# Output stage of a transformer layer: tiles in pairs, in another order, with shared small operations

## The reference

```
x = layernorm(x + attention(x, Wqkv, Wo))          # 16 heads of 16, rotary positions
normed = x * rsqrt(mean(x^2) + 1e-8) * norm_weight
shared = relu(normed @ sw1 + sb1) @ sw2 + sb2      # hidden size 1024
comb   = the two best of 8 experts a row, by sigmoid(normed @ router_w.T), weights normalised
routed = sum over the two: comb * (relu(normed @ ew1[e] + eb1[e]) @ ew2[e] + eb2[e])
out    = layernorm(x + shared + routed)            # (v - mean) / sqrt(var + 1e-5)
```

## Time and profile before

| | |
|---|---|
| median of 3 runs | 1319.67 us (1319.3 to 1321.2) |
| the profiled execution's own time | 1322.56 us |
| its span in the trace | 1320.7 us |
| mean granted clock of TensorE | 0.97 |
| busy: TensorE, VectorE, ScalarE, GpSimd | 1220.1, 1028.5, 970.0, 578.8 us |
| `combine` | about 1234 us to the end, 87 us |
| last product of TensorE | 1291.4 us |

### The profile page before, as it was taken

How to read it: one execution, slowest core, us unless ns; L and a number is a source line. 1 busy time by engine, 2 the same in 40 slices (tenths; PEclk the granted TensorE clock), 3 DMA queues, 4 the chain that set the end, 5 groups by cost and what they waited for, 6 DMA issues and landing times.

```text
span 1320.7 us, 29483 instructions
## 1 busy us (share of the span) xinstructions
PE 1220.1 (92%) x9377; PEld 933.8 (71%) x9440; DVE 1028.5 (78%) x2009; ACT 970.0 (73%) x1938; POOL 578.8 (44%) x572
## 2 busy tenths in 40 slices
PE   4799999999999999869999969999999999999991
PEld 3444444444444444238899969999999999999891
DVE  5788887888788878629756638888888888888798
ACT  4599998999899999747744427767767677677684
POOL 5332322232223210007436645666666666666560
PEclk9899999999999999999899989999999999999996
DMA  9300101010000000442022246777777777776344
GB/s 298 107 18 2 34 9 29 2 34 2 20 2 18 2 18 18 141 135 69 14 89 90 85 132 222 251 251 238 245 238 242 241 239 239 245 249 203 127 146 139
DMA packets 125412, 161.25 MB, mean 122 GB/s; under 512 B 17088, under 2 KB 108224, under 8 KB 125312
## 3 DMA queue, kind: packets, MB, share of 16 engines
q1 hardware_dynamic: 118496, 141.25, 33.2%
q0 software_dynamic: 6816, 18.75, 3.7%
HBM read 122.06 MB, written 37.52 MB: 121 GB/s over the span
## 4 chain that ended last, share of the span: by engine, by line
PE 75%; DMA 9%; DVE 8%; issue 3%; ACT 3%; POOL 1%; SPq 0%; another core or an unknown queue 0%; ACTq 0%; DVEq 0%; POOLq 0%
PE att_psV L387 9%; PE att_psA L330 9%; PE att_psB L340 8%; DMA slots_x<-sent_rows,all_slot 6%; PE exp_psU L1581 5%; PE exp_psU L1583 5%; PE exp_psU L1582 5%; PE exp_psD L1566 5%; PE exp_psD L1567 5%; PE exp_psD L1568 5%; PE att_psT L354 4%; PE att_psX L408 2%; PE att_psX L410 2%; PE att_psX L409 2%; PE exp_psT L1554 1%
## 5 line engine op out<-in xcount | busy, mean ns | idle before, releaser
L529 DVE TENSOR_REDUCE att_mx<-att_psA 128x1 f32<-128x512 f32 x512 | 337.6, 682 | 76.3 <-PE att_psA L330 74.9
L445 ACT ACTIVATE att_prob<-att_psB 128x512 f32<-128x512 f32 x512 | 299.3, 599 | 54.1 <-PE att_psB L340 40.0
L1626 ACT ACTIVATE exp_psU<-exp_psU,ew_b 128x256 f32<-128x256 f32 x312 | 126.9, 445 | 132.2 <-PE exp_psU L1583 132.2
L330 PE MATMUL att_psA<-att_qk 96*128 96x512 bf16 x512 | 197.5, 388 | 6.4 <-DVE att_mx L529 2.4
L340 PE MATMUL att_psB<-att_qk 128*128 128x512 bf16 x449 | 172.4, 386 | 14.1 <-issue 5.4
L1566 PE MATMUL exp_psD<-exp_w2h,exp_hh 128*128 128x256 f32 x624 | 175.7, 282 | 0.0
L1581 PE MATMUL exp_psU<-exp_xh,exp_w1h 128*128 128x256 f32 x624 | 173.7, 278 | 1.4 <-DVE exp_xl L1650 1.4
L1583 PE MATMUL exp_psU<-exp_xh,exp_w1l 128*128 128x256 f32 x624 | 173.3, 278 | 0.0
L1582 PE MATMUL exp_psU<-exp_xl,exp_w1h 128*128 128x256 f32 x624 | 173.3, 278 | 0.0
L1567 PE MATMUL exp_psD<-exp_w2l,exp_hh 128*128 128x256 f32 x624 | 172.4, 276 | 0.0
L1568 PE MATMUL exp_psD<-exp_w2h,exp_hl 128*128 128x256 f32 x624 | 172.3, 276 | 0.0
(11 more groups left out here) (203 smaller groups left out, 3240.3 us busy)
## 6 DMA issues: line engine op xcount, KB each, us to landing
ew_w<-ew SPq DMA_DIRECT2D x40, 1024.0 KB, 7.0
exp_w<-ew SPq DMA_DIRECT2D x38, 1024.0 KB, 7.1
slots_x<-pre_acc SPq DMA_DIRECT2D x13, 780.0 KB, 10.5
pre_spare<-slots_x SPq DMA_DIRECT2D x39, 260.0 KB, 5.5
out_g<-rows_y SPq DMA_DIRECT2D x32, 256.0 KB, 3.1
ew_b<-eb SPq DMA_DIRECT2D x39, 128.0 KB, 5.9
pre_spare<-xT SPq DMA_DIRECT2D x8, 512.0 KB, 4.5
attn_rows<-att_ob SPq DMA_DIRECT2D x8, 512.0 KB, 2.8
```

Of the source, the lines that this page charges most:

```text
L330: pe.matmul(psA[A_BANK[n % U]][:, :], r[:, 0, qt * P:(qt + 1) * P], r[:, 1, :], start=True, stop=True).then_inc(s_amm, 1)
L445: act.activation(prob[:, n % PR, :], psB[B_BANK[n % U]][:, :], ACT.Exp, scale=SCALE).then_inc(s_exp, 1)
L529: dve.reduce_max(mx[:, g % 2, n % U:n % U + 1], psA[A_BANK[n % U]][:, :], AX_X).then_inc(s_max, 1)
```

## The change

`combine` now works on pairs of tiles, numbered k = 0 to 15 in the order ORDER = 0, 1, 2, 11, 3, 4, 12, 5, 6, 13, 7, 8, 14, 9, 10, 15 (pair p holds tiles 2p and 2p+1; 11 to 15 are the blocks whose shared product is made here).

- VectorE: the first sum of both tiles, one wait, the second sum of both, one wait, the statistics of both, one wait, two aggregates. One reciprocal and one scaled mean over two columns serve both. They belong to pair k-2 up to k = 8, to pairs 7 and 8 at k = 9, and to pair k-1 after that. The add of block n stands directly before its own pair. All eight `hidden_lo` of block 0 come before `rows_lo` of block 1; `rows_lo` of block 2 comes after pair 0.
- ScalarE: one root for two tiles, in slots given by the list ROOT; two normalisings in slots given by NORM. The relus and `rows_hi` keep their slots, and roots of a slot come before its normalisings.
- GpSimd: the same instructions in the same order.
- SP: the load of pair i+6 waits until pair i is summed, and the stores follow three pairs behind.
- y, o and the small buffers hold six pairs in place of eight tiles.

```diff
+    R, LAG = 6, 2
+    ORDER = list(range(3))
+    for n in range(NB):
+        ORDER += [EARLY + n] + list(range(2 * n + 3, min(2 * n + 5, EARLY)))
+    ROOT = [6, 8, 10, 12, 14, 15, 18, 19] + [12 + k for k in range(8, PAIRS)]
+    NORM = [10, 12, 14, 16, 18, 19, 20, 21] + [13 + k for k in range(8, PAIRS)]
...
+            def add_up(k):
+                p, r = ORDER[k], k % R
+                dve.wait_ge(s_g[r], 32 * (k // R + 1))
+                if k >= R:
+                    dve.wait_ge(s_o, 2 * (k - R + 1))
+                if p >= EARLY:
+                    dve.wait_ge(shared.added, p - EARLY + 1)
+                for t in range(2):
+                    i = 2 * p + t
+                    ins = dve.scalar_tensor_tensor(y[:, r, t, :], g[:, r, 0, t, :], m.gate[:, 0, i:i + 1], m.acc[:, i, :], ALU.mult, ALU.add)
+                link(ins)
+                for t in range(2):
+                    i = 2 * p + t
+                    ins = dve.scalar_tensor_tensor(y[:, r, t, :], g[:, r, 1, t, :], m.gate[:, 1, i:i + 1], y[:, r, t, :], ALU.mult, ALU.add)
+                ins.then_inc(s_y, 1)
+                dve.wait_ge(s_y, k + 1)
+                dve.bn_stats(st[:, r, 0, :], y[:, r, 0, :])
+                link(dve.bn_stats(st[:, r, 1, :], y[:, r, 1, :]))
+                for t in range(2):
+                    dve.bn_aggr(mv[:, r, t, :], st[:, r, t, :]).then_inc(s_var, 1)
+
+            def scale(k):
+                r = k % R
+                dve.wait_ge(s_sd, k + 1)
+                link(dve.reciprocal(sd[:, r, 1, :], sd[:, r, 0, :]))
+                dve.scalar_tensor_tensor(sd[:, r, 2, :], mv[:, r, :, 0], -1.0, sd[:, r, 1, :], ALU.mult, ALU.mult).then_inc(s_nm, 1)
...
             shared.rows_lo(dve, Nth(0))
-            for slot in range(LAG + TILES + 2):
...
+            for h in range(shared.HC):
+                shared.hidden_lo(dve, Nth(0), h)
+            rows_ahead(1)
+            for k in range(PAIRS):
+                n = ORDER[k] - EARLY
+                if n >= 0:
+                    shared.add(dve, Nth(n))
+                add_up(k)
+                if k == 0:
+                    rows_ahead(2)
+                if n >= 0:
+                    rows_ahead(n + 3)
+                if LAG <= k < PAIRS - 7:
+                    scale(k - LAG)
+                if k == PAIRS - 7:
+                    scale(k - 2)
+                if k >= PAIRS - 7:
+                    scale(k - 1)
+            scale(PAIRS - 1)
...
+            def root(k):
+                r = k % R
+                act.wait_ge(s_var, 2 * (k + 1))
+                act.activation(sd[:, r, 0, :], mv[:, r, :, 1], ACT.Sqrt, bias=eps[:, 0:1]).then_inc(s_sd, 1)
...
+            for i in range(PAIRS + 3):
+                if i + R < PAIRS:
+                    sp.wait_ge(s_y, i + 1)
+                    load(i + R)
+                if i >= 3:
+                    k = i - 3
+                    for t in range(2):
+                        row = (2 * ORDER[k] + t) * P
+                        sp.wait_ge(s_o, 2 * k + t + 1)
+                        sp.dma_start(out[row:row + P, :], o[:, k % R, t, :]).then_inc(s_st[k % R], 16)
```

More of the change, by code:

```diff
@@ L1703, in combine @@
     TILES = T // P
[L1704 to L1707, removed]
+    PAIRS = TILES // 2
+    EARLY = m.early_blocks
+    NB = PAIRS - EARLY
+    R, LAG = 6, 2
+    HP = m.sb1.shape[1] // 2
+    SLOTS = NB * HP
+    ORDER = list(range(3))
+    for n in range(NB):
+        ORDER += [EARLY + n] + list(range(2 * n + 3, min(2 * n + 5, EARLY)))
+    assert sorted(ORDER) == list(range(PAIRS))
+    ROOT = [6, 8, 10, 12, 14, 15, 18, 19] + [12 + k for k in range(8, PAIRS)]
+    NORM = [10, 12, 14, 16, 18, 19, 20, 21] + [13 + k for k in range(8, PAIRS)]
     with ExitStack() as ctx:
@@ L1711, in combine @@
         eps = given.eps
[L1712 to L1720, removed]
+        g = a.sb("g", [P, R, 2, 2, D], F32)
+        y = a.sb("y", [P, R, 2, D], F32)
+        o = a.sb("o", [P, R, 2, D], F32)
+        st = a.sb("st", [P, R, 2, 6], F32)
+        mv = a.sb("mv", [P, R, 2, 2], F32)
+        sd = a.sb("sd", [P, R, 3, 2], F32)
+        shared = Shared(a, m, 2 * EARLY, buffers=2)
+        s_g = [a.sem(f"outputs_loaded{i}") for i in range(R)]
         s_var = a.sem("variance")
@@ L1728, in combine @@
         block = pr.block
[L1730 to L1733, removed]
         @block.gpsimd
         def _(pool):
-            for slot in range(TILES + 2):
-                n, h = divmod(2 * (slot - 1), shared.HC)
-                if n == 1 and h == 0:
+            for n in range(1, NB):
+                if n == 1:
                     pool.wait_ge(shared.lo_ready, shared.HC)
-                if 1 <= n < NB:
+                for h in range(shared.HC):
                     shared.hidden_lo(pool, Nth(n), h)
-                    shared.hidden_lo(pool, Nth(n), h + 1)
         @block.vector
@@ L1754, in _, with rows_ahead @@
+            def scale(k):
[3 more added lines that the diff above has]
+                dve.scalar_tensor_tensor(sd[:, r, 2, :], mv[:, r, :, 0], -1.0, sd[:, r, 1, :], ALU.mult, ALU.mult).then_inc(s_nm, 1)
+            def rows_ahead(n):
+                if n < NB:
+                    shared.rows_lo(dve, Nth(n))
             pr.after_last(dve)
             shared.rows_lo(dve, Nth(0))
-            for slot in range(LAG + TILES + 2):
[L1757 to L1784, removed]
@@ L1796, in _, with normalise @@
         def _(act):
+            def root(k):
+                r = k % R
+                act.wait_ge(s_var, 2 * (k + 1))
+                act.activation(sd[:, r, 0, :], mv[:, r, :, 1], ACT.Sqrt, bias=eps[:, 0:1]).then_inc(s_sd, 1)
+            def normalise(k):
+                r = k % R
+                act.wait_ge(s_nm, k + 1)
+                if k >= R:
+                    act.wait_ge(s_st[r], 32 * (k // R))
+                for t in range(2):
+                    act.activation(o[:, r, t, :], y[:, r, t, :], ACT.Identity, bias=sd[:, r, 2, t:t + 1], scale=sd[:, r, 1, t:t + 1]).then_inc(s_o, 1)
             shared.rows_hi(act, Nth(0))
-            for slot in range(LAG + TILES + 3):
+            for slot in range(NORM[-1] + 1):
                 n, h = divmod(2 * slot, shared.HC)
-                if n < NB:
+                if slot < SLOTS:
                     shared.relu(act, Nth(n), h)
@@ L1804, in _ @@
                     shared.rows_hi(act, Nth(n + 1))
[L1805 to L1815, removed]
+                for k in range(PAIRS):
+                    if ROOT[k] == slot:
+                        root(k)
+                for k in range(PAIRS):
+                    if NORM[k] == slot:
+                        normalise(k)
         @block.sync
         def _(sp):
-            y_quad = rows_y[SPARE:].rearrange("(k q t p) d -> k q p t d", k=2, t=QT, p=P)
+            y_pair = rows_y[SPARE:].rearrange("(k q t p) d -> k q p t d", k=2, t=2, p=P)
             pr.after_last(sp)
@@ L1823, in _, with load @@
                 sp.wait_ge(*landed)
[L1825 to L1838, removed]
+            def load(k):
+                for plane in range(2):
+                    sp.dma_start(g[:, k % R, plane], y_pair[plane, ORDER[k]]).then_inc(s_g[k % R], 16)
+            for k in range(R):
+                load(k)
+            for i in range(PAIRS + 3):
[4 more added lines that the diff above has]
+                    k = i - 3
+                    for t in range(2):
+                        row = (2 * ORDER[k] + t) * P
+                        sp.wait_ge(s_o, 2 * k + t + 1)
+                        sp.dma_start(out[row:row + P, :], o[:, k % R, t, :]).then_inc(s_st[k % R], 16)
             for r in range(R):
-                sp.wait_ge(s_st[r], 16 * (TILES // R))
+                sp.wait_ge(s_st[r], 32 * ((PAIRS - 1 - r) // R + 1))
 class Carried:
```

## The result

The changed kernel takes 1315.99 us (median of 20 runs, 1313.05 to 1319.65) against 1318.97 for the kernel before in the same rounds: ratio 0.9978, interval [0.997, 0.9987], about 2.9 us faster. Two later sets of runs, in which both kernels took some 3% longer (medians of 1354 to 1363 us), gave 0.9982 [0.9952, 1.0012] and 0.9966 [0.9943, 0.9989]. The profiled execution took 1318.61, its span is 1316.8.

A forecast was written before the change was run, and what follows sets the result against it. VectorE's queue was taken to bound the last stage. Pairing saves 0.62 us a pair, 9.9 for 16; walked with a late start, GpSimd losses and the tail, span falls 6.7 to 1314.0, median 1313.0; 8-in-10 range 1310.8 to 1317.8.

The forecast's parts named there:

- main case: Whole kernel: span falls 6.7 us to 1314.0, median 1313.0, own range 1311.5 to 1315.5; chance 70%.
- rival (c): TensorE's clock falls to half for about 3.4 us in the longer gap, costing 1.7 us: median 1314.7; chance 7%.
- loss to GpSimd: VectorE's two-input operations are held up while GpSimd splits hidden values: 0.57 us a GpSimd pair, bounds 0 and 1.48.
- price of a pair: VectorE with GpSimd quiet: two tiles together cost 3.12 us in place of 3.74, 0.62 saved a pair.
- own wait: VectorE waiting for its own last result: 0.12 us each, three fewer a pair, 0.35 us of the saving.
- rival (a): VectorE's waits cost nothing, only dropped instructions save: span 1319.2, down 1.5 us, median 1318.2; chance 10%.
- (b): Four adds in a row meet GpSimd's lock: slower above 1.04 us a GpSimd pair, median 1325.8 at 1.48; chance 5%, milder form 8%.
- thin cover of TensorE's fifth block: The block, due at 1276.2, needs VectorE's row split, due at about 1275.8: 0.4 us of cover.
- floor: VectorE's scaling of pair 6 must await a root ScalarE issues in slot 18, ready at 1284.45; VectorE just meets it.
- TensorE begins at 1243.60, 1.45 late, and so does all that follows it: Stage start: the later row split delays TensorE's second block and following ScalarE and GpSimd work 1.45 us; gap 1.4 to 2.9.
- pair 9: VectorE: 3.56 us with its block add, two scalings 0.54, one last GpSimd loss 0.57, done at 1289.5.
- Pairs 1 to 8: VectorE: 27.0 us of work, stretched by GpSimd's 0.57 every 2.72 us to 34.2, ending at 1284.5.

The follow-up runs named there:

- changed kernel's second: The changed kernel unaltered, profiled again in a later set of runs: stage 82.93 us, ratio to the kernel before 0.9982.
- early split: Changed kernel with the row split of block 1 moved before hidden splits 6 and 7, as in the kernel before: stage 79.86 us, ratio 0.9949.
- filled gap: Changed kernel, row split still late, with 22 products nobody reads put into TensorE's gap before its second block: stage 81.27 us, ratio 0.9941.
- early roots: Changed kernel with the roots of pairs 6, 7 and 8 one slot earlier on ScalarE (17, 18, 19): stage 81.29 us, ratio 0.9942.
- both early: Changed kernel with block 1's row split before hidden splits 6 and 7 and roots of pairs 6 to 8 one slot earlier: stage 77.86 us, ratio 0.9938.
- filled kernels: 22 unread products in TensorE's gap, in the changed kernel (stage 81.27 us) and in the kernel before with the late row split (88.51 us).
- waits put back: Changed kernel with a wait after each tile's first add, second add and statistics, three more a pair: stage 86.45 us, ratio 0.9992.
- changed kernel's first and third profile: The changed kernel unaltered, in its original profile and another from a later set: stages 83.79 and 83.74 us, ratios 0.9978 and 0.9966.
- natural order: Changed kernel with pairs summed in order 0 to 15, shared adds and row splits keeping their places: stage 83.50 us, ratio 0.9970.

## Why the prediction was wrong

The direction and the range held, the size did not: 6.7 us forecast, 3.4 in the profiled stage and 2.9 by the runs. The measured 1315.99 lies above the main case's own range (1311.5 to 1315.5) and above rival (c)'s 1314.7. That it lies in the wider range is in part luck: the upper end was kept for a loss to GpSimd that did not come, and the longer steps were in no term.

Right, within 0.1 us or nearly: the price of a pair (3.12, measured 3.03) and of an own wait (0.12, measured 0.13), so rival (a) is refuted for these operations. The Trainium skill ("VectorE: DVE Perf Modes", section "The DRAIN you can't avoid") reports for eight copies that a wait behind each cost nothing; the trace doesn't agree for these adds, which take 0.88 us without and 1.01 with a wait between them. TensorE's second block 10.04 us into the stage, 10.05 forecast. There was no reversal by GpSimd's lock (b): the three groups that answer to rows 6 are

```profile
L1771 DVE SCALAR_TENSOR_TENSOR out_y<-out_g,all_gate,out_y 128x256 f32<-128x256 f32 x32 | 18.5, 618 | 0.6
L1767 DVE SCALAR_TENSOR_TENSOR out_y<-out_g,all_gate,pre_acc 128x256 f32<-128x256 f32 x32 | 16.0, 539 | 0.7
...
L1784 DVE SCALAR_TENSOR_TENSOR out_sd<-out_mv,out_sd 128x2 f32<-128x2 f32 x16 | 3.7, 231 | 0.6
```

38.2 us, where 16 x (0.88 + 0.88) + 16 x 0.16 = 30.7 would be without GpSimd: 7.5 lost, 0.54 for each of the 14 GpSimd pairs after VectorE's second start, against 0.57 forecast. That the order is free and that the loads are early held too. The thin cover of TensorE's fifth block gave way by 0.42 us in five profiles (the changed kernel's second, early split, filled gap, early roots, both early), and as predicted that only moved the floor: with the filled gap root 6 stood 51.4 us into the stage, 0.5 behind the forecast 50.9.

Wrong: the step "TensorE begins at 1243.60, 1.45 late, and so does all that follows it". What follows came later by much more: root 6 stood 53.9 us into the stage and not 50.9, and VectorE waited 2.26 us for it, which is the prediction's own sign that the floor and not VectorE sets the time. 1.6 us of the 3.0 are the dip: with the gap filled and the steps equal, the stage is 1.66 us shorter. 1.4 are worked out from the longer steps, 0.1177 for 0.1133 us over the 37 us between; no experiment took them away by themselves. Between two profiles of the same kernel they made only 0.9 us of stage, since with the shorter steps the fifth block's 0.42 us comes in. The other 0.3 us of the 3.3 by which the stage is longer than forecast are the net of smaller terms, the largest of them pair 9, which met GpSimd for 0.85 us in place of 0.57.

Rival (c) named the dip and its length, got 7%, and was priced at 1.7 us against the main case, which is what the filled kernels show; I argued it away by how long the clock held after TensorE's last product. That was one stretch of standing after 49 us of work; this gap comes 5.7 us after another of 1.61 us. Whether it is that earlier gap that makes the difference, no run here shows.

One term erred the other way. Pairs 1 to 8 took VectorE 33.4 us, with the filled gap as in the changed kernel, and not 34.2. It gave nothing, since the floor holds VectorE there: even with the gap filled it waits 1.37 us for root 6, where the prediction had it "just meet" the floor.

The second fault is in the placing. The late row split costs the same 3.1 us in both kernels (87.15 to 90.21; 82.93 to 79.86 the other way), in both 1.4 by the late start and 1.7 by the dip, though nothing of what the change is about needs it. Without it and with the roots a slot earlier the pairing gives 87.15 - 77.86 = 9.3 us, near the 9.9 that its VectorE work is worth. The changed kernel keeps 3.4 to 4.2 of them; 3.1 go into the late split and about 2 into the slot of root 6 (79.86 - 77.86).

## What to carry to other kernels

When an engine's queue is rewritten, walk the few instructions ahead of the loop too: one operation moved behind two others gave back a third of the gain, since three engines hang on it. Price a new gap of TensorE with the dip of its clock (1.7 us here), and where a gap can't be closed, fill it. When the bounding engine becomes faster, schedules that other engines have by hand must move with it: a wait that it newly has is the sign of a slot written too late, as root 6 here.

## What the runs showed of the hardware

In seven profiles TensorE stood for 1.61 us, worked for 5.7 to 5.9 and stood for 2.67 to 2.86; all seven then show 3.4 us at 1.2 GHz. With 0.36 to 1.41 us in place of the second stand, none of seven does. The clock fell between 0.1 us before the end of the gap (waits put back) and 1.3 us behind it (changed kernel).

At a granted clock of 1.00 TensorE issued the same products 0.1133 us apart in some stretches and 0.1177 in others. From the dip to the end it was 0.1177 in the changed kernel's first and third profile, with the natural order and in the kernel before with the late split; with the early roots it became 0.1177 only 46 us into the stage; with the early row split and the waits put back it was 0.1177 in the first block, ahead of the gap, and 0.1133 later. So the longer steps don't need a dip, and a dip doesn't bring them each time. They cost up to 0.9 us of this stage; no run here says what sets them, and it stays open.

Two adds of 128 x 256 on VectorE took 0.88 us side by side and 1.01 with a wait for the first between them.
